# Language-model layer on one Trainium2 core: Newton roots on DVE, weight scales in two groups, squares on ScalarE

## The reference

```python
h = take(W.T, x)                                    # 2048 rows of 128
# attention: a recurrence over 512 time steps, hidden size 128
xn = layernorm(h); xb = xn @ B.T
s_t = tanh(s_{t-1} @ A.T + xb_t)                    # for each of 4 sequences
a  = states @ C.T
h  = h + (sigmoid(a @ Wg.T + bg) * a) @ Wo.T + bo
# experts: each row goes to the one of 8 experts with the greatest logit
xf = layernorm(h); e = argmax(xf @ gate_w.T)
y  = (silu(xf @ w1[e].T) * (xf @ w3[e].T)) @ w2[e].T
y  = y + gelu(xf @ sw1.T) @ sw2.T                   # shared layers
h  = h + y
```

## Time and profile before

| | |
|---|---|
| median of 3 runs | 208.74 us (206.99, 208.74, 209.55) |
| the profiled execution | 208.46 us |
| its span, first to last instruction | 206.7 us |
| busy: PE, DVE, ScalarE, POOL | 148.5, 137.8, 92.1, 83.5 us |
| step 0 of the recurrence starts | 12.71 us |
| last step's tanh ends | 70.5 us |
| shared layers end, expert blocks begin | about 141 us |

### The profile page before, as it was taken

How to read it: one execution, slowest core, us unless ns; L and a number is a source line. 1 busy time by engine, 2 the same in 40 slices (tenths; PEclk the granted TensorE clock), 3 DMA queues, 4 the chain that set the end, 5 groups by cost and what they waited for, 6 DMA issues and landing times.

```text
span 206.7 us, 3176 instructions
## 1 busy us (share of the span) xinstructions
PE 148.5 (72%) x998; PEld 105.2 (51%) x998; DVE 137.8 (67%) x364; ACT 92.1 (45%) x199; POOL 83.5 (40%) x80
## 2 busy tenths in 40 slices
PE   0158899888888788766598742257999999999610
PEld 0046777666666467532266521044677776776410
DVE  0366667996899769958999950012688888887710
ACT  2001122333599537769877600003666666665300
POOL 4788848000000014320007777700046666666660
PEclk9999999999999999999999985555899999999995
DMA  5544349940000001120001231222003222223240
GB/s 159 180 140 135 107 144 302 385 169 0 0 2 3 0 3 51 52 102 0 3 2 38 94 102 52 54 35 88 3 5 35 29 25 29 25 29 32 29 38 0
DMA packets 9955, 13.83 MB, mean 67 GB/s; under 512 B 1936, under 2 KB 4752, under 8 KB 9936
## 3 DMA queue, kind: packets, MB, share of 16 engines
q1 hardware_dynamic: 5904, 9.91, 14.2%
q0 software_dynamic: 4032, 3.67, 11.4%
HBM read 10.17 MB, written 3.41 MB: 66 GB/s over the span
## 4 chain that ended last, share of the span: by engine, by line
PE 46%; ACT 14%; issue 14%; POOL 12%; DVE 11%; DMA 1%; POOLq 0%; ACTq 0%
PE bank L587 13%; PE bank L427 8%; POOL emb_rows L341 7%; PE bank L530 7%; PE bank L612 6%; ACT states L627 5%; PE bank L600 4%; ACT w_hl L637 2%; POOL rstd L349 2%; ACT w_hl L639 2%; PE bank L476 2%; PE bank L425 2%; DVE stats L740 2%; POOL rstd L360 2%; DVE w_sb L885 2%
## 5 line engine op out<-in xcount | busy, mean ns | idle before, releaser
L378 POOL DMA_INDIRECT out<-out_blk,row_of x20 | 31.1, 1557 | 34.1 <-DVE out_blk L1019 34.1
L627 ACT ACTIVATE states<-bank 128x128 f32<-128x128 f32 x56 | 15.5, 278 | 43.7 <-PE bank L427 31.8
L427 PE MATMUL bank<-states,sq_sb 128*128 128x128 f32 x112 | 30.0, 355 | 5.5
L587 PE MATMUL bank<-w_hl,xblk_t 128*128 x120 | 30.7, 394 | 0.7 <-issue 0.7
L427 PEld LDWEIGHTS bank<-states,sq_sb 128*128 128x128 f32 x112 | 19.8, 221 | 14.3 <-ACT states L627 14.3
L425 PE MATMUL bank<-x_in,sq_sb 128*128 128x128 f32 x112 | 25.7, 316 | 1.3 <-issue 0.7
L530 PE MATMUL bank<-sw_hl,states 128*128 128x128 f16 x128 | 16.3, 240 | 13.0 <-issue 13.0
L360 POOL TENSOR_TENSOR rstd<-vareps,cst 128x2 f32<-128x2 f32 x8 | 5.5, 692 | 48.0 <-DVE vareps L746 48.0
L425 PEld LDWEIGHTS bank<-x_in,sq_sb 128*128 128x128 f32 x112 | 20.1, 225 | 1.8 <-issue 1.7
L530 PEld LDWEIGHTS bank<-sw_hl,states 128*128 128x128 f16 x128 | 11.5, 107 | 18.1 <-issue 16.2
L707 ACT ACTIVATE w_sb<-bank,factor 128x512 f32<-128x512 f32 x20 | 13.8, 688 | 13.1 <-PE bank L587 13.1
(11 more groups left out here) (132 smaller groups left out, 282.6 us busy)
## 6 DMA issues: line engine op xcount, KB each, us to landing
w_sb<-w SPq DMA_DIRECT2D x24, 256.0 KB, 6.3
x_rows<-norm SPq DMA_DIRECT2D x4, 256.0 KB, 2.3
out<-attn_out SPq DMA_DIRECT2D x4, 256.0 KB
sw_sb<-sw SPq DMA_DIRECT2D x2, 256.0 KB
cst<-consts SPq DMA_DIRECT2D x1, 420.0 KB
sq_sb<-sq SPq DMA_DIRECT2D x1, 384.0 KB
out<-out_blk,row_of POOLq DMA_INDIRECT x20
emb_rows<-emb,tok_sb POOLq DMA_INDIRECT x16
```

What stands on the lines that cost most here:

```text
L378: pool.indirect_dma_start(out=out, out_offset=bass.IndirectOffsetOnAxis(ap=row_of[:, k:k + 1], axis=0), in_=out_blk[k % RING][:], in_offse ...
L427: pe.matmul(pre, at, states[:, i * COLS:(i + 1) * COLS], start=False, stop=True).then_inc(pre_ready, 1)
L587: mm = pe.matmul(hb[:], xblk_t[:, k % 3, b * P:(b + 1) * P], w[:, bass.ds(e * INNER + a * EXPERTS * INNER, INNER)], start=(j == 0), stop=( ...
L627: act.activation(states[:, (i + 1) * COLS:(i + 2) * COLS], bank[i % 2][:, 0:COLS], ACT.Tanh).then_inc(state_ready, 1)
```

## The change

1. POOL's loop issues all sixteen gathers in one go. DVE computes the inverse roots of pairs 0 to 3 itself, from a bit trick and three Newton steps (`inverse_root`, eleven dependent small instructions), for pairs (0, 1) together and then (2, 3) together. POOL's power remains for pairs (4, 5), (6) and (7), behind all gathers.
2. The copy to `x_in` moves from DVE to ScalarE (`bring`), behind a tanh.
3. The weights' scales are made in two groups. The first (w1, sw1, sw2, gate) still uses maxima on DVE; PE turns it at step 18 and spreads it at step 20. The second (w3, w2) uses the sum of squares of each part instead of the maximum, computed on ScalarE with the accumulator, one part behind each tanh of steps 14 to 29; DVE halves the exponent of the greatest sum, which bounds the greatest value from above. PE turns it at step 31 and spreads it at step 33.
4. DVE's order behind the first group: splits of sw1, sw2, gate, the high half of w1, the second group's three small instructions, low half of w1 in three slices (3, 3 and 2 experts) with the second group's steps between them. ScalarE's high halves stay at steps 38 to 53.
5. All eight low halves of w3 and five of w2 stand ahead of the closing check, the last three of w2 behind it. None is left in the shared layers.

```diff
-            for n in range(PAIRS + 2):
-                if n < PAIRS:
-                    for t in pair_tiles(n):
-                        pool.indirect_dma_start(out=emb_rows[:, t, :], ...).then_inc(gathered[n], 16)
-                if n >= 2:
-                    ...
-                    pool.wait_ge(var_ready, n - 1)
-                    pool.tensor_tensor(rstd[:, t0:t0 + 2], vareps[:, t0:t0 + 2], cst[:, C_POW:C_POW + 2], ALU.pow
-                                       ).then_inc(rstd_ready, 1)
+            for n in range(PAIRS):
+                for t in pair_tiles(n):
+                    pool.indirect_dma_start(out=emb_rows[:, t, :], ...).then_inc(gathered[n], 16)
+            pool.wait_ge(small_in, 80)
+            for k, pairs in enumerate(LATER):          # (4, 5), (6,), (7,)
+                ...
+                pool.wait_ge(var_ready, k + 1)
+                pool.tensor_tensor(rstd[:, ts], vareps[:, ts], cst[:, C_POW:C_POW + 2 * len(pairs)], ALU.pow
+                                   ).then_inc(rstd_ready, 1)
```

```diff
 # tensor
-                if i == MAX_STEP:                       # 32, and the spread at 34
-                    pe.wait_ge(max_ready, 1)
-                    pe.transpose(bank[5][0:WEIGHTS, 0:P], max_rows[:], ident).then_inc(max_turned, 1)
+                for b, (at_step, group) in enumerate(zip(MAX_STEPS, (FIRST, SECOND))):   # (18, 31)
+                    n = group.stop - group.start
+                    if i == at_step:
+                        pe.wait_ge(max_ready, b + 1)
+                        pe.transpose(bank[5][0:n, 0:P], max_rows[:, group], ident).then_inc(max_turned, 1)
+                    if i == at_step + 2:
+                        pe.wait_ge(diag_ready, b + 1)
+                        pe.matmul(bank[6][:, 0:n], ones[0:n, :], max_diag[b][0:n, 0:n], start=True, stop=True
+                                  ).then_inc(max_spread, 1)
 # scalar
+            def bring(n):
+                p0 = pair_tiles(n)[0]
+                act.wait_ge(norm_turned, n + 1)
+                act.activation(x_at[:, p0:p0 + PPP, :, PADK:XB], bank[2 + n % 2][:, 0:PC]..., ACT.Copy
+                               ).then_inc(x_ready, 1)
+
+            bring(0)
             for i in range(STEPS):
                 ... tanh ...
+                if i % PPP == 0 and i // PPP + 1 < PAIRS:
+                    bring(i // PPP + 1)
+                j = i - SQUARE_STEP                     # 14
+                if 0 <= j < 2 * PARTS:
+                    act.wait_ge(w_in[PARTS + j], 16)
+                    if j >= 1:
+                        act.wait_ge(squared, j)
+                    act.activation(attn_out[:, 0:4, :]..., (w3_sb, w2_sb)[j // PARTS][:, part(j)], ACT.Square,
+                                   accum_out=part_sum[:, j // PARTS, j % PARTS:j % PARTS + 1]).then_inc(squared, 1)
```

```diff
 # vector
+            def inverse_root(y, x, ts):
+                y, x, a, b = (v[:, ts] for v in (y, x, gain_a, gain_b))
+                then_wait(dve.tensor_scalar(half_bits[:, ts], x.bitcast(I32), 1, None, ALU.logical_shift_right))
+                then_wait(dve.tensor_scalar(y.bitcast(I32), half_bits[:, ts], -1.0, float(RSQRT_SEED), ALU.mult, ALU.add))
+                for _ in range(3):
+                    then_wait(dve.scalar_tensor_tensor(out=a, in0=y, scalar=-0.5, in1=x, op0=ALU.mult, op1=ALU.mult))
+                    then_wait(dve.tensor_tensor(b, a, y, ALU.mult))
+                    then_wait(dve.scalar_tensor_tensor(out=y, in0=b, scalar=1.5, in1=y, op0=ALU.add, op1=ALU.mult))
+            for pairs in EARLY:                         # (0, 1), (2, 3)
+                ins, ts = variance(pairs)
+                then_wait(ins)
+                inverse_root(rstd, vareps, ts)
+                for n in pairs:
+                    normed(n)
...
-            for j in range(3 * PARTS):
-                ins = greatest_part(j)
+            for j in range(PARTS):
+                dve.wait_ge(w_in[j], 16)
+                ins = greatest(part_max[:, j:j + 1], w1_sb[:, part(j)])
...
+            dve.wait_ge(squared, 2 * PARTS)
+            then_wait(dve.tensor_reduce(max_rows[:, SECOND], part_sum[:], AX.X, ALU.max))
+            root = max_rows[:, SECOND].bitcast(I32)
+            then_wait(dve.tensor_scalar(sum_bits[:], root, 1, None, ALU.logical_shift_right))
+            dve.tensor_scalar(root, sum_bits[:], 1.0, float(ROOT_BIAS), ALU.mult, ALU.add).then_inc(max_ready, 1)
+            w1_low(slice(0, 3 * INNER))
+            turned_greatest(1, 2)
+            w1_low(slice(3 * INNER, 6 * INNER))
+            powers_of_two(1, SECOND)
...
+            w1_low(slice(6 * INNER, 8 * INNER)).then_inc(w_split, 1)
-            for j in range(EXPERTS - 4):
+            for j in range(EXPERTS):
                 w3_low(j)
+            for j in range(EXPERTS - 3):
+                w2_low(j)
             ... closing check ...
-            for j in range(EXPERTS - 4, EXPERTS):
-                w3_low(j)
+            for j in range(EXPERTS - 3, EXPERTS):
+                w2_low(j)
...
             for n in range(8, GROUPS * IC):
                 act_low_half(n)
-                w2_low(n - 8)
```

More of the change, by code:

```diff
@@ L52 @@
 PC = 2 * P
-MAX_STEP = 32
-HIGH_STEP = MAX_STEP + 6
+EARLY = ((0, 1), (2, 3))
+LATER = ((4, 5), (6,), (7,))
+RSQRT_SEED = 0x5F3759DF
+SQUARE_STEP = 14
+MAX_STEPS = (18, 31)
+HIGH_STEP = 38
 FIRST_TILE = -WARM % CHUNK
@@ L59 @@
 WEIGHTS = 6
+W1, SW1, SW2, GATE, W3, W2 = range(WEIGHTS)
+FIRST, SECOND = slice(0, 4), slice(4, 6)
+ROOT_BIAS = 127 << 22
 BLOCKS = TILES + EXPERTS - 1
@@ L132, in build @@
         gate_hl = sb("gate_hl", [P, 2, EXPERTS], F16)
-        part_max = sb("part_max", [P, 3, PARTS])
+        part_max = sb("part_max", [P, PARTS])
+        part_sum = sb("part_sum", [P, 2, PARTS])
+        sum_bits = sb("sum_bits", [P, 2], I32)
         max_rows = sb("max_rows", [P, WEIGHTS])
-        max_col = sb("max_col", [WEIGHTS, 1])
-        max_diag = sb("max_diag", [WEIGHTS, WEIGHTS])
+        max_col = [sb(f"max_col{i}", [4, 1]) for i in range(2)]
+        max_diag = [sb(f"max_diag{i}", [4, 4]) for i in range(2)]
         max_all = sb("max_all", [P, WEIGHTS])
@@ L155, in build @@
         vareps = sb("vareps", [P, TILES])
-        rstd = sb("rstd", [P, TILES])
+        rstd, gain_a, gain_b = (sb(n, [P, TILES]) for n in ("rstd", "gain_a", "gain_b"))
+        half_bits = sb("half_bits", [P, TILES], I32)
         norm_rows = sb("norm_rows", [P, 4, P])
@@ new lines, in variance @@
+            def variance(pairs):
+                tiles = [t for n in pairs for t in pair_tiles(n)]
+                for n in pairs:
+                    dve.wait_ge(gathered[n], 32)
+                    for t in pair_tiles(n):
+                        ins = dve.bn_stats(stats[:, t, :], emb_rows[:, t, :])
+                then_wait(ins)
+                for t in tiles:
+                    ins = dve.bn_aggr(meanvar[:, t, :], stats[:, t, :])
+                then_wait(ins)
+                ts = slice(tiles[0], tiles[-1] + 1)
+                return dve.tensor_scalar(vareps[:, ts], meanvar[:, ts, 1], EPS, None, ALU.add), ts
@@ new lines, in normed @@
+            def normed(n):
+                if n >= 2:
+                    dve.wait_ge(norm_turned, n - 1)
+                normalise(norm_rows, emb_rows, meanvar, rstd, pair_tiles(n), n, norm_ready)
+            for pairs in EARLY:
+                ins, ts = variance(pairs)
+                then_wait(ins)
+                inverse_root(rstd, vareps, ts)
+                for n in pairs:
+                    normed(n)
+            dve.wait_ge(wgc_done, 1)
+            dve.tensor_copy(wgc[:], bank[4][:, 0:P]).then_inc(wgc_ready, 1)
@@ new lines, in _, with turned_greatest @@
+            for k in range(len(LATER) + 1):
+                if k < len(LATER):
+                    variance(LATER[k])[0].then_inc(var_ready, 1)
+                if k >= 1:
+                    dve.wait_ge(rstd_ready, k)
+                    for n in LATER[k - 1]:
+                        normed(n)
+            def turned_greatest(b, n):
+                dve.wait_ge(max_turned, b + 1)
+                then_wait(dve.tensor_reduce(max_col[b][0:n, :], bank[5][0:n, 0:P], AX.X, ALU.max))
+                dve.tensor_scalar(max_diag[b][0:n, 0:n], ident[0:n, 0:n], max_col[b][0:n, :], None, ALU.mult).then_inc(diag_ready, 1)
@@ new lines, in powers_of_two @@
+            def powers_of_two(b, group):
+                dve.wait_ge(max_spread, b + 1)
+                then_wait(dve.tensor_copy(max_all[:, group], bank[6][:, 0:group.stop - group.start]))
+                then_wait(dve.tensor_scalar(max_exp[:, group], max_all[:, group].bitcast(I32), 0x7F800000, None, ALU.bitwise_and))
+                then_wait(dve.tensor_scalar(max_exp_in[:, group], max_exp[:, group], float(97 << 23), float(167 << 23), ALU.max, ALU.min))
+                then_wait(dve.tensor_scalar(scale_i[:, group], max_exp_in[:, group], -1.0, float(268 << 23), ALU.mult, ALU.add))
```

(10 more changed lines are left out.)

101 lines of the change are left out of this document (37 added, 64 removed).

## The result

The changed kernel took 215.16 us (median of 4 runs, 213.95 to 216.66). The kernel before, run beside it on the same chip, took 207.95 (206.99 to 209.55). The ratio is 1.034, interval 1.023 to 1.045: **slower**, by some 7 us, where 208.0 within 205.0 to 211.2 was forecast.

A forecast was written before the change was run, and what follows sets the result against it. Start-up gathers until about 33 us, then the 56 recurrence steps, then PE's issue stretch without named cause were taken to bound the kernel. From 208.46, -1.9 + 0.3 + 0.1 + 0.6 - 0.1 + 0.55 = -0.45 gave 208.0 us, range 205.0 to 211.2.

The forecast's parts named there:

- Start and pace: Start-up to step 14: step 0 2.3 us later, then a faster pace, step 14 at 31.6; -1.9 us.
- DVE work inside the issue stretch doesn't move the end: Near the end of the shared layers, PE's issue stretch until 137.57 us: DVE work inside it doesn't move the end.
- the low halves' leaving the shared layers: Shared layers: eight low halves leave DVE, but PE fills the pace alone; 0 us, bounds 0 and -1.3.
- Rival 4: The issue stretch or a new queue wait grows by over 5 us: 213 us and more; chance 0.06.
- The stretch itself: Shared layers' end: 14.4 us of PE "issue" in 18 gaps before L530, until 137.57; expected to keep its length.
- Rival 3: Shared layers' end: the issue stretch changes; 188 us if it went, 198 for half of it; chance 0.10.
- the squares: Steps 14 to 29: one ScalarE square behind each tanh, bounds nothing and 1.8 us with overlaps; +0.3 us taken.
- rival 2: Steps with squares: square isn't in tanh's table, so 32 loads of 1.28 us, 249 us; chance 0.03.
- step 33: Recurrence: second turned maximum stands behind three eighths of w1's low half, so PE waits at step 33; +0.6 us.
- the closing check: End of the recurrence: five w2 low halves ahead make the check 0.93 us later, PE waits before step 55; +0.55 us.
- no wait at step 18: Recurrence: DVE's first maxima ready at 34.5 us against 35.5 for step 18; no wait, 0.3 us if step 14 comes at 30.7.
- the gain of 2.8 us: Start-up: the bound with PE at full speed from pair 4, step 14 at 30.7 us against 33.54.

The follow-up runs named there:

- best_newton: Changed kernel with embedding gathers spaced by powers, maxima at steps 23 and 35, reordered low halves, idle power behind every second expert gather; 194.33 us, ratio 0.938 to the kernel before.
- mended: Changed kernel with second group's maxima turned before any low half of w1, and four instead of five w2 low halves ahead of the closing check; 213.68 us, ratio 1.027.
- lows_back: Changed kernel with its two waits taken out by order and the low halves of w2 made in the shared layers again; 211.78 us, ratio 1.018.
- spaced_blocks: Kernel before, with an idle 0.7 us power on POOL behind every second gather for the experts; 193.81 us, ratio 0.939.
- start_only: Kernel before with the change's start alone: gathers in one row, Newton roots, x_in copied by ScalarE; 210.08 us, ratio 1.015.
- after: The whole changed kernel, against the kernel before; 215.16 us, ratio 1.034.
- rest_only: Changed kernel with the old start: everything of the change but its start; 214.37 us, ratio 1.034 to the kernel before.
- spaced_start: Changed kernel with a 0.7 us idle power on POOL behind each pair of embedding gathers from the third on; 214.3 us, ratio 1.036 to the kernel before.

## Why the prediction was wrong

- **Start and pace, -1.9 forecast, +2.0 measured: the step that failed.** The terms took every engine's instruction times as the trace gave them beside the old start, in which powers stood between the gathers, and asked only what each instruction waits for. The first matmul of step 0 came at 15.29 (15.0 forecast). The first of step 14 was forecast at 31.6 and its tanh came at 36.56, where 34.60 goes with 33.54. Taking the powers out made POOL put out gathers at 1.25 us without a break, and that held everybody up, ScalarE for 6 us. With the gathers spaced again (best_newton) the idea gave 0.3 us by step 14.
- **"DVE work inside the issue stretch doesn't move the end": wrong.** I priced the low halves' leaving the shared layers at 0 to -1.3. It cost some 1.8 us, with 1.4 us either way (ratios 1.027 and 1.018 of mended and lows_back), most likely through POOL's gathers. Rival 4, a longer issue stretch, named the place, at 0.06 and without a cause; it asked for over 5 us, and the stretch grew by 3.0.
- **The stretch itself** was left without a cause and carried over one for one. Rival 3 priced its going at 188 to 198 us; spaced_blocks took 193.8. It was the largest single stretch in this kernel, and a wait without a named cause should have been looked into before it was carried over.
- **Right**: the squares (0.3 forecast, 0 measured: with 0.62 and 0.19 us the tanh still follow at 0.86); no table load between tanh and square (rival 2); step 33 (+0.6, measured 0.57); the closing check (+0.55, measured 0.46); no wait at step 18.
- **PE's speed at the start** changed sooner, and it didn't help. Before, the float32 matmuls that wait for nothing start 0.43 us apart until 33.2 us, and L425's two instructions together take 0.64 us at 30.34 and 0.39 at 34.40. In the changed kernel L434, the same matmul, takes 0.64 us at 16.71 and 0.39 at 29.74, and from 29.52 to 29.74 the distance is 0.22. The trace's first record of the granted clock, full speed, is at 18.52 there; it fell at 21.94, within the stop, and rose again at 28.77. Before, the first record is at 33.43. The slices of the page print the time ahead of the first record as full, which is why didn't show PE's slow start. Full speed some 5 us earlier (28.77 against 33.43) saved less than the stop had cost. What lets PE's speed rise no run shows, and none shows the gain of 2.8 us that the -1.9 leans towards: step 14 came 2.0 us later in the changed kernel, and in best_newton 0.3 us earlier than with the old start.
- **The ends of the sum**: "206.2 to 209.6" doesn't come out of the parts. Their own ends (start -2.8 and -0.3, squares 0 and 1.8, low halves -1.3 and 0, the other terms as they stand) give 205.5 to 211.1 us.
- **Not in the sum**: PE's clock later on. In the profiled execution half clock in attention took 1.4 to 1.9 us and near 107 us 0.8. How much of it the medians hold stays open.

By ratios, in steps from the kernel before: start 1.5% (start_only), squares and groups without their waits 0.3% more (lows_back), the low halves' place 0.9% (mended), the two waits and what follows on them 0.8% (after). They add up to the 3.4% because each run builds on the one before, and each has an uncertainty of half a per cent or more. The last three steps are no larger than that or little more. In another order the shares differ: the whole change without its start is at 3.4% too (rest_only).

## What to carry to other kernels

When several engines pause at once with "issue" or "remote" beside their names, look at what GpSimd is putting out at that time before you price anything in that stretch; spreading its indirect gathers with something 0.7 us long was worth 12.5 us in the kernel before (206.3 to 193.8), while copies of 0.2 to 0.5 us were worth nothing. Before you take work off an engine that nobody waits for, ask what that work had been slowing down: here, it seems, it paced the gathers. And don't move operations out from between gathers without a run of that alone.

## What the runs showed of the hardware

- 20 indirect gathers of GpSimd at 1.25 to 1.37 us from one another make the stretch from row_in to the experts 13 to 18 us longer than at 1.69 us, and at 1.45 us 7 us longer (the table). At the start, 16 gathers at 1.25 us held PE, DVE and ScalarE up from some 15 us after the first until 2.7 us after the last (the tanh of step 2 at 25.26, with the row broken in spaced_start at 18.71). The gathers' own transfers didn't fall behind (before and after, over 2.1 to 2.8 us after each one's start, 3.2 to 3.7 for the last two).
- Beside VectorE's low halves of 128x512 a gather takes 1.02 us (before, start_only, lows_back) instead of 0.94 (after, mended), and one in each of the first three 1.67.
- ScalarE's square of 128x512 with a sum takes 0.62 us and its read-out 0.19; sixteen of them in turn with tanh needed no table load (after, 36 to 51 us).
